# A six-stage network on one core: first-stage scores, merges and a state product moved ahead, weights loaded before context

## The reference

```python
# stage 1: three iterations of slot attention with a GRU; P is a context of 1601 rows for each of 8 batches
Pn = rmsnorm(P, input_norm_w); k_proj = Pn @ Wk.T; v_proj = Pn @ Wv.T
for _ in range(3):
    q_proj = rmsnorm(slots, slot_norm_w) @ Wq.T
    attn = softmax(einsum('bkd,bmd->bkm', q_proj, k_proj) * SCALE, axis=-2)
    attn = attn / (sum(attn, axis=-1, keepdims=True) + EPS)
    updates = einsum('bkm,bmd->bkd', attn, v_proj)
    slots = gru_cell(updates, slots, wih, whh, bih, bhh)
# stage 2: ... layer norm, state-space scan, linear, then
out = res2 + linear(gelu(linear(layer_norm(x1), ffn1)), ffn2)
# stage 4: attention of the 64 tokens on the same context, 16 heads, masked
w = softmax(where(keep, q k^T / sqrt(HD), min)); out = (w v) @ Wo + bo
```

## Time and profile before

| | us |
|---|---|
| median of 3 runs | 3411.62 (3409.67 to 3412.1) |
| profiled execution, its own time | 3412.18 |
| its span | 3410.4 |
| granted TensorE clock, mean | 0.946 |
| TensorE busy | 2971.7 (87%) |
| chain that ended last | TensorE 75%, DVE 9%, DMA 6% |

### The profile page before, as it was taken

The page is one execution under the profiler, slowest core; times in us unless marked ns, Lnnn a source line. Parts: engine busy times, 40 slices in busy tenths (PEclk is TensorE's granted clock), DMA queues, the critical chain, the costliest instruction groups (busy, mean ns, idle before and its releaser), DMA issues.

```text
span 3410.4 us, 37825 instructions
## 1 busy us (share of the span) xinstructions
PE 2971.7 (87%) x14622; PEld 2028.6 (59%) x14622; DVE 1341.5 (39%) x2005; ACT 1039.8 (30%) x1724; POOL 268.0 (8%) x273
## 2 busy tenths in 40 slices
PE   7767889887888779999999979988988988978787
PEld 3325437354574448888888746866866866844432
DVE  4335363456731433333333344244244244244301
ACT  3223212123340433433433323233233233233210
POOL 1110110130010000000000011101101101000000
PEclk9888989998999879999999989999999999989799
DMA  8662794941021012222222210100100100021097
GB/s 358 257 248 101 279 379 161 359 194 50 13 74 62 1 62 99 97 90 96 98 98 98 86 40 20 40 22 18 40 22 18 40 23 17 22 105 37 25 394 307
DMA packets 62216, 387.97 MB, mean 114 GB/s; under 512 B 5696, under 2 KB 12096, under 8 KB 32704
## 3 DMA queue, kind: packets, MB, share of 16 engines
q1 hardware_dynamic: 26640, 190.57, 14.8%
q0 software_dynamic: 29024, 192.23, 14.3%
q10 hardware_dynamic: 6480, 4.20, 0.4%
HBM read 381.72 MB, written 5.24 MB: 113 GB/s over the span
## 4 chain that ended last, share of the span: by engine, by line
PE 75%; DVE 9%; DMA 6%; issue 5%; ACT 3%; POOL 2%; DVEq 0%; SPq 0%; ACTq 0%; POOLq 0%
PE PS L373 9%; PE PS L375 9%; PE PS L374 9%; PE PS L544 4%; PE PS L1590 4%; PE PS L296 4%; PE PS L519 3%; PE PS L1529 3%; PE PS L1545 3%; PE PS L1531 3%; PE PS L1530 3%; PE PS L1547 3%; PE PS L1546 3%; DMA PR<-in_ctxN 3%; PE PS L1577 2%
## 5 line engine op out<-in xcount | busy, mean ns | idle before, releaser
L373 PE MATMUL PS<-X_high,W_high 128*128 128x512 f32 x576 | 225.9, 392 | 27.6 <-POOL W_part L1029 27.6
L374 PE MATMUL PS<-X_low,W_high 128*128 128x512 f32 x576 | 225.5, 391 | 0.0
L375 PE MATMUL PS<-X_high,W_part 128*128 128x512 f32 x576 | 225.3, 391 | 0.0
L374 PE MATMUL PS<-H_low,W_high 128*128 128x512 f32 x576 | 224.2, 389 | 0.0
L373 PE MATMUL PS<-H_high,W_high 128*128 128x512 f32 x576 | 224.2, 389 | 0.0
L375 PE MATMUL PS<-H_high,W_part 128*128 128x512 f32 x576 | 224.2, 389 | 0.0
L1037 DVE TENSOR_TENSOR W_part<-ring,W_high 128x2048 fp32r<-128x2048 f32 x63 | 147.0, 2334 | 188.6 <-ACT W_high L1004 188.6
L1004 ACT ACTIVATE W_high<-ring 128x2048 fp32r<-128x2048 f32 x72 | 136.9, 1914 | 255.0 <-PE PS L375 255.0
L1716 DVE TENSOR_TENSOR RB<-PS,rows 128x512 f32<-128x512 f32 x104 | 71.9, 691 | 292.7 <-PE PS L1547 292.7
L1043 DVE TENSOR_TENSOR H_low<-T,H_high 128x512 fp32r<-128x512 f32 x144 | 99.6, 692 | 221.2 <-ACT H_high L1024 221.2
L1529 PE MATMUL PS<-C_high,W_part 128*128 128x448 f32 (+1 forms) x512 | 180.8, 353 | 6.1 <-DVE T L1735 5.2
(11 more groups left out here) (313 smaller groups left out, 5826.8 us busy)
## 6 DMA issues: line engine op xcount, KB each, us to landing
ring<-in_experts SPq DMA_DIRECT2D x96, 1024.0 KB, 4.8
ring<-in_tiles SPq DMA_DIRECT2D x39, 1024.0 KB, 4.8
RA<-in_ctxT POOLq DMA_DIRECT2D x20, 1792.0 KB, 8.2
RA<-in_ctxT POOLq DMA_DIRECT2D x20, 1536.0 KB, 6.9
T<-in_ctxN POOLq DMA_DIRECT2D x24, 1024.0 KB, 13.7
RA<-in_experts SPq DMA_DIRECT2D x24, 1024.0 KB, 12.6
RC<-in_ctxN POOLq DMA_DIRECT2D x12, 1792.0 KB, 12.2
RB<-in_ctxT POOLq DMA_DIRECT2D x12, 1792.0 KB, 13.7
```

Source lines behind the costliest of these rows:

```text
L373: pe.matmul(ps, a, xh, start=start, stop=False)
L374: pe.matmul(ps, a, xl, start=False, stop=False)
L375: return pe.matmul(ps, b, xh, start=False, stop=stop)
```

## The change

- Load order: POOL waits until `wq` and `wk` have landed, then loads the first pair's `ct`, then its `cn` (before: `cn` first, no wait).
- Iteration 0, pairs 1 to 3: the next pair's scores, the turn of the last pair and the first half of a merge stand ahead of the pair's transposes. ACT's squares and root stand ahead of `updates_out`.
- Every iteration: the first GRU product (`whh0`) stands ahead of the last pair's `updates`: in iteration 0 also ahead of its transposes, in the others behind them. Its high and low parts are made one pair earlier. The GRU order is now whh0, whh2, wih0, wih2, whh1, wih1, with `gh` and z in banks 4 to 7 and `gx` in 0 to 3. The turn of the last pair now stands inside the second product, after two of its four outputs.
- Stage 2: the first feed-forward weight's high part is made ahead of the norm (`first_high_act`).
- Stage 4: every `values(g, k)` except the last moves behind one more transpose block, `values(g, 0)` also behind `scores(g+1, 1)`; ACT's two `exps` stand ahead of `turn_out` 4 and 6 instead of 6 and the end; both `normalise` stand ahead of DVE's second `turn_out` and of `out`.

TensorE, iteration 0, second pair (b = 1), before: totals of pair 0, transposes, turn, then the next scores (the first rows of 64), with the merge behind them.

```diff
             for it in range(3):
                 order += [(f"s1.{it}.G", "s1.G")] if it else []
-                order += [(f"s1.{it}.{w}{g}", AT[f"s1.whh{g}"] if w == "whh" else f"s1.m{g}") for g in (0, 2, 1) for w in ("whh", "wih")]
+                order += [(f"s1.{it}.{w}", AT[f"s1.{w}"] if w[:3] == "whh" else f"s1.m{w[3]}") for w in ("whh0", "whh2", "wih0", "wih2", "whh1", "wih1")]
         if 2 in stages:
             order += [(n, AT[n]) for n in ["s2.out"] + [f"s2.ffn{1 if x[0] == 'a' else 2}_{x[1]}" for x in EXPERT]]
...
-        GRU = [("whh0", "r", 0, True, False), ("wih0", "r", 0, False, True), ("whh2", "gh", 0, True, True),
-               ("wih2", "gx", 4, True, True), ("whh1", "z", 0, True, False), ("wih1", "z", 0, False, True)]
+        GRU = [("whh0", "r", 0, True, False), ("whh2", "gh", 4, True, True), ("wih0", "r", 0, False, True),
+               ("wih2", "gx", 0, True, True), ("whh1", "z", 4, True, False), ("wih1", "z", 4, False, True)]
+        DBANK = [1] * (PAIRS - 1) + [5]
+        MBANK = [(7, 4, 7, 4), (4, 7, 7, 4), (4, 7, 7, 4)]
...
+            pool.wait_ge(*at.done("s1.wq"))
+            pool.wait_ge(*at.done("s1.wk"))
+            for h in (0, 1):
+                for u in (0, 1):
+                    transposed("s1.0", 0, u, h)
             for h in (0, 1):
                 for u in (0, 1):
                     natural("s1.0", 0, u, h)
-            for h in (0, 1):
-                for u in (0, 1):
-                    transposed("s1.0", 0, u, h)
             for it in range(3):
...
+            def merged(j, kcs):
+                g = GATES[j]
+                for kc in kcs:
+                    k = MBANK[j][kc]
...
+                if kcs[-1] == KC - 1:
+                    at.same(f"s1.wih{g}.used")
+                    at.same("s1.wv.used")
...
+                    k = DBANK[b]
+                    pe.wait_ge(*at.done(bank_reader[k]))
                     for h in (0, 1):
-                        mm = pe.matmul(PS[:, 1, 448:449], asum[h], C["ones"][:, 0:1], start=(h == 0), stop=(h == 1))
...
-                for h in (0, 1):
-                    scores(0, h)
-                for b in range(PAIRS):
-                    for h in (0, 1):
-                        transposes(b, h)
-                    if b:
-                        turn(b - 1)
-                    if b + 1 < PAIRS:
-                        for h in (0, 1):
-                            scores(b + 1, h)
-                        if it == 0:
-                            merged(GATES[b])
-                    for h in (0, 1):
-                        updates(b, h)
-                    totals(b)
-
-                for k, (w, tag, banks, first, last) in enumerate(GRU):
+                def recurrent(k):
+                    w, tag, banks, first, last = GRU[k]
                     xh, xl, ready = (SLH, SLL, "state") if w[:3] == "whh" else (SNH, SNL, "update")
...
+                        if k == 1 and oc == 2:
+                            turn(PAIRS - 1)
...
-                        if k == 0 and oc == 0:
-                            turn(PAIRS - 1)
...
+                def ahead_of(b):
+                    if b == PAIRS:
+                        recurrent(0)
+                        return
+                    for h in (0, 1):
+                        scores(b, h)
+
+                ahead_of(0)
+                for b in range(PAIRS):
+                    if it == 0 and b:
+                        ahead_of(b + 1)
+                        turn(b - 1)
+                        if b + 1 < PAIRS:
+                            merged(b, (0, 1))
+                    for h in (0, 1):
+                        transposes(b, h)
+                    if it or b == 0:
+                        if b:
+                            turn(b - 1)
+                        ahead_of(b + 1)
+                    if it == 0 and b + 1 < PAIRS:
+                        merged(b, (2, 3) if b else range(KC))
+                    for h in (0, 1):
+                        updates(b, h)
+                    totals(b)
+                for k in range(1, len(GRU)):
+                    recurrent(k)
...
+                if it == 0:
+                    squares(0, 0)
+                    squares(0, 1)
+                    root(0)
+                scores_out(0, 0)
+                scores_out(0, 1)
+                for b in range(PAIRS):
+                    merging = it == 0 and b + 1 < PAIRS
+                    if it == 0 and b:
+                        squares(b, 0)
+                        squares(b, 1)
+                        root(b)
+                    if b:
+                        updates_out(b - 1)
+                    if merging and b:
+                        merged_out(b, (0, 1))
+                    exps(b, 0)
+                    exps(b, 1)
+                    if b + 1 < PAIRS:
+                        scores_out(b + 1, 0)
+                        scores_out(b + 1, 1)
+                    if merging:
+                        merged_out(b, (2, 3) if b else range(KC))
+                    if b == PAIRS - 2:
+                        for c in range(KC):
+                            act.activation(SLH[:, c, :], SL[:, c, :], ACT.Copy).then_inc(*at.step(f"{L}.state.high{c}"))
+                        high(0)
                 high(1)
+                high(2)
                 updates_out(PAIRS - 1)
                 act.wait_ge(*at.own())
                 for c in range(KC):
                     act.activation(SNH[:, c, :], UP[:, c, :], ACT.Copy).then_inc(*at.step(f"{L}.update.high{c}"))
-                high(2)
+                high(3)
...
+                    if b == PAIRS - 2:
+                        if it == 0:
+                            dve.wait_ge(*at.done(f"s1.m{GATES[-1]}.stored"))
+                        for c in range(KC):
+                            dve.wait_ge(*at.done(f"{L}.state.high{c}"))
+                            dve.tensor_tensor(SLL[:, c, :], SL[:, c, :], SLH[:, c, :].bitcast(FP32), ALU.subtract).then_inc(*at.step(f"{L}.state.low{c}"))
+                        low(0)
                     if b + 1 < PAIRS:
...
-                if it == 0:
-                    dve.wait_ge(*at.done(f"s1.m{GATES[-1]}.stored"))
-                for c in range(KC):
-                    dve.wait_ge(*at.done(f"{L}.state.high{c}"))
-                    dve.tensor_tensor(SLL[:, c, :], SL[:, c, :], SLH[:, c, :].bitcast(FP32), ALU.subtract).then_inc(*at.step(f"{L}.state.low{c}"))
-                low(0)
+                low(1)
                 normalise(PAIRS - 1)
-                low(1)
+                low(2)
...
+        def first_high_act(act, at, w):
+
+            act.wait_ge(*at.done(w(0)))
+            act.activation(high_at(0)[:, :, :], wt(w(0))[:, :, :], ACT.Copy).then_inc(*at.step(w(0) + ".high"))
...
-            high(0)
+            if inloop:
+                high(0)
...
             for c, b0, b1 in dve_shares:
                 act.activation(Y2[:, c, b0 * S:b1 * S], Y2[:, c, b0 * S:b1 * S], ACT.Silu).then_inc(*at.step("s2.silu"))
+            first_high_act(act, at, FFN)
             norm_act(act, at, "s2.ln2", R2, "eps5", xc=N2)
...
                     transposes(g, 0, 0)
                     transposes(g, 0, 1)
                     transposes(g, 1, 0)
-                    values(g, 0)
                     if g + 1 < KC:
                         scores(g + 1, 1)
                     transposes(g, 1, 1)
+                    values(g, 0)
                     transposes(g, 2, 0)
+                    transposes(g, 2, 1)
                     values(g, 1)
-                    transposes(g, 2, 1)
                     transposes(g, 3, 0)
+                    transposes(g, 3, 1)
                     values(g, 2)
-                    transposes(g, 3, 1)
                     values(g, 3)
             at.same("s4.wk.used", "s4.v3.3"); at.same("s4.wv.used", "s4.v3.3")
             bank_reader.update({k: f"s4.m3.1.{k // 2}" for k in range(4)})
@@ -1666,12 +1698,10 @@
                 exps(0, 1)
                 for g in range(KC):
                     for i in range(2 * NG):
-                        if i == 5 and g + 1 < KC:
-                            exps(g + 1, 0)
+                        if i in (4, 6) and g + 1 < KC:
+                            exps(g + 1, i // 2 - 2)
                         if i not in BY_DVE:
                             turn_out(g * 2 * NG + i)
-                    if g + 1 < KC:
-                        exps(g + 1, 1)
 
         def s4_dve(dve, at):
 
@@ -1753,11 +1783,11 @@
                         turn_out(g * 2 * NG + i)
                     if g + 1 < KC:
                         normalise(g + 1, 0)
+                    if g + 1 < KC:
+                        normalise(g + 1, 1)
                     for i in BY_DVE[1:]:
                         turn_out(g * 2 * NG + i)
                     out(b, g)
-                    if g + 1 < KC:
-                        normalise(g + 1, 1)
```

53 lines of the change are left out of this document (12 added, 41 removed).

## The result

| | before | after |
|---|---|---|
| median | 3411.7 us (3409.67 to 3412.1) | 3320.97 us (3314.53 to 3322.44) |
| profiled execution, its span | 3410.4 us | 3312.8 us |
| TensorE busy; mean granted clock | 2971.7 us; 0.946 | 2965.2 us; 0.957 |

The ratio is 0.9732, 95% interval 0.9715 to 0.9748, 91 us less by the medians; 3325 was forecast. The profiled execution was the fastest of the changed kernel, so the comparison of the two traces (97.6 us) shows the gain some 7 us larger than the medians do. A second set of five runs of the same kernel had the median 3315.59.

What follows compares the result with a forecast made beforehand. It took TensorE's work to bound stage 4 (busy 929 of 1020 us) and chains of waits across engines and loads stage 1. Terms 9 + 21 + 4 + 11 + 9.6 - 4.2 + 9 + 28 = 87.4 off 3412.18 gave 3325; range 3300 to 3364.

Steps and rivals of the forecast that it cites:

- load order: Start of iteration 0: with POOL holding the context back, the first product starts 9.1 us earlier; 9 us less, bounds 4 to 10.
- rings of pairs 1 and 2: Iteration 0, from one pair's last natural loads to the next's: 51 us instead of 61.56; 10.6 won twice, 21 less.
- last pair and state product, iteration 0: Less collision with SP's weight loads, 4 us (0 to 6); first GRU product wholly inside the load wait, 11 us.
- state product, iteration 1: First GRU product moves into TensorE's idle time ahead of the last updates: 9.6 us less, 8 if starting at low clock.
- iteration 2: End of stage 1: fifth product waits for POOL's powers and DVE's low part; ends 4.2 us later instead of 9.6 earlier.
- stage 2: The first weight's parts are made beside the linear product, shortening TensorE's idle time: 9.0 us less (8 to 9.2).
- stage 4: Eight batches at -4.1 us each, -33; taken as -28 in case the clock falls; bounds -33 and +4.
- A: Rival: TensorE's clock falls in the quarters of stage 4, which gives +4 instead of -28; 3357 us, chance 0.24.
- B: Rival: loads get in each other's way, lengthening iteration 0's rings by up to 5.5 us each; 3345 us, chance 0.12.
- D: Rival: the state product does not help in iteration 1 either, something it needs being late; 20 us lost, 3345, chance 0.08.
- C: Rival: slower than before, stage 4's new ring exceeding 12.45 us by over 4.2 per quarter; 3421 at 17 us, chance 0.04.

Runs made afterwards that it cites:

- the experiment that removes it: Changed kernel with ScalarE's copies of the turned updates and first two merge products ahead of the root, iteration 0, pairs 1 and 2: 3305.67 us, ratio 0.9696.

## Why the prediction was right

| step | forecast less, us | measured less, us |
|---|---|---|
| load order | 9 | 9.5 (issue at 111.67 for 121.16); alone 8.5 |
| rings of pairs 1 and 2 | 21 | 9.1 + 10.4 |
| last pair and state product, iteration 0 | 4 + 11 | 14.1 (43.1 less the lines above) |
| state product, iteration 1 | 9.6 | 8.9 |
| iteration 2 | -4.2 | -2.2 |
| stage 2 | 9.0 | 8.7 |
| between stages 2 and 4 | 0 | -1.7 |
| stage 4 | 28 | 40 |
| behind stage 4 | 0 | 0.8 |
| sum | 87.4 | 97.6 of the spans, 91 of the medians |

The measured column is read from the two traces, of which the second was the fastest execution; by the median the forecast was 4 us off. Three parts were also shown by runs of their own: stage 4 (39.2 us alone), the load order (8.5 alone) and the state product (29.9 when undone). The new order of the rings and the part in stage 2 were not run alone; for them the traces before and after speak.

- **Load order.** Right in size, and that the context is late next was right too. The reason was only half right: the prediction credited the weights' early landing, but in the traces the iteration ends at the same time without the two waits. Without them the first transposes follow scores that end late, and start at 67.71; with them they follow the squares of the natural half, and start at 68.20. So the size was right partly by luck.
- **Rings.** Forecast 51, measured 52.43 and 51.32. The stop ahead of the second merge quarter came as argued (5.96 us of it in the first ring, 4 forecast), with the low clock behind it: that quarter took 5.90 us, the one before it 3.60. Its cost is shown by the experiment that removes it: 7.9 and 6.5 us.
- **Last pair.** The prediction expected the natural load to land sooner; it did (14.1 us after its issue instead of 16.73). It left out the semaphore that `state_low` waits for, the store of the merge, although that wait stands in the diff and the store's 18.56 us in the trace before. So the product did not lie "wholly" in the wait for the load: it started 8.16 us late and ended with it. That cost next to nothing only because the load ended at the same time; the right number is luck here.
- **Iterations 1 and 2.** Both as argued, though undoing the product costs 6.6 us in iteration 1 and not 8.9, so that line of the table is not the product's alone. In iteration 2 the wait is 11.90 us (14 forecast), since POOL's powers took 28.65 us instead of 30.63.
- **Stage 4** is the term that was mis-sized. The links were right within 0.3 us: first exponential at 6.9 us after the last values (7.0 forecast), second at 9.05 (9.2), copy at 12.1 (12.3), last values at 12.45 (12.65). Eight batches at -4.1 should have been at -5.1: the 0.2 us per quarter were not there, the 0.6 more for the first quarter was 0.45 (89.92 for 89.47), and the last quarter was 5.5 us shorter, not 5.2. The other 5 us I had taken off for the clock, which did not fall.
- **Rivals.** A did not happen in the change, but 0.86 us more of wait brought it on at 15 of 24 waits, at 1.5 us each. B did not: the loads of pairs 1 and 2 took 12.42 and 11.46 us (11.26 and 11.62 before). D fell by the experiment that undoes the product (6.6 us more in iteration 1). C was far off: the quarters stayed at 12.45 us.

## What to carry to other kernels

When an instruction moves, list everything that its inputs' buffers still wait for, stores as well: the store behind the state's low part was a wait nobody had counted. Where two chains meet, price an edit together with what else ends there: holding SP's loads back was worth 0.8 us by itself, and 10.8 once other edits had made the store's chain the later one. And after a reordering ask of each operation that now stands ahead of a needed copy who waits for it: here the answer was next to nobody, and 29 us lay in it.

## What the hardware showed that was not expected

**The clock near its edge.** Ahead of stage 4's last values, 1.61 us waits were followed by a fall of the clock in none of 24 in each of seven traces (the changed kernel twice and the five with edits elsewhere: 888.0 to 888.2 us from the first values to the last in all) and in 2 of 24 in the kernel with the stage 4 part alone. At 2.47 us it fell at 15 of 24. After the waits of 1.98 us in the kernel before, between transposes, it fell at all eight. So the length of a wait does not settle it alone, and the same wait in one program can go either way; that what stands around it counts as well is likely, but no run changed the surroundings at the same length.

**GpSimd beside VectorE.** POOL's low part of the first feed-forward weight took 8.83 us before and half of it after, with the same operands (8.82 or 8.83 in the three traces that have stage 2 of the kernel before, 4.50 or 4.51 in the eleven that have the changed one). In the kernel before, VectorE had two operations with two inputs in SBUF beside it:

```profile
939.30 2.49 DVE L1141 TENSOR_TENSOR X<-X,T 128x512 f32<-128x512 f32 x4
941.71 2.28 DVE L1037 TENSOR_TENSOR W_part<-ring,W_high 128x2048 fp32r<-128x2048 f32 x1
```

```profile
939.52 8.83 POOL L1029 TENSOR_TENSOR W_part<-ring,W_high 128x2048 fp32r<-128x2048 f32 x1 [171.11 <-ACT W_high L1004]
```

and after:

```profile
856.20 4.51 POOL L1060 TENSOR_TENSOR W_part<-ring,W_high 128x2048 fp32r<-128x2048 f32 x1 [139.92 <-ACT W_high L1025]
```

VectorE was through at 943.99, 4.47 us after POOL's start; from there 4.36 us were left, about the whole 4.51. So POOL stood still meanwhile. The Trainium skill, "SBUF — State Buffer", section on who interferes with whom, calls the port pair of SBUF that both share an exclusive lock. The trace agrees, with 4.47 us of standing still ahead of 4.36 of work. The powers show it smaller: 28.65 us while VectorE waits for 20 us of them, 32.68 where it works beside them (in the run with the reduction later).

**A small store in heavy traffic.** 256 KB from ScalarE's queue took 17.36 us beside 4 MB of SP's and 6.8 MB of POOL's loads (17.4 to 23.6 in the traces with this traffic, those of the kernel before among them), and 5.97 with 3 MB of SP's held back, when it landed before POOL's loads were issued. The same store of an earlier merge, at 190.66, took 2.44 us.
